# A gated delta rule on one core: the order of all engines' work around one (head, sequence) pair

## The chip, the core and the metric

The kernel runs on one core of a Trainium2 chip. The time is the device time of that core in microseconds. The core has TensorE (PE; its weight loads are shown as PEld), VectorE (DVE), ScalarE (ACT), GpSimd (POOL) and SyncE (SP), which here only starts DMA transfers. Each engine executes its own list of instructions strictly in the order in which the kernel writes them, and the lists are tied together by semaphores.

## The reference

Input x has 8 sequences of 512 rows with 256 features. The computation is:

```
h  = layernorm(x)
q,k,v = silu(causal_conv4(h @ Wqkv)) in 16 heads of 128;  z = h @ Wz
beta = sigmoid(h @ Wb);  g = -exp(A_log) * softplus(h @ Wa + dt_bias)
q, k = l2norm(q) / sqrt(128), l2norm(k)
for t:  M = exp(g_t) M;  M = M + k_t (v_t - k_t M) beta_t;  o_t = q_t M
o  = rmsnorm(o) * norm_w * silu(z);  x = x + layernorm(o @ Wout)
x  = x + layernorm(W3 relu(W2 relu(W1 layernorm(x) + b1) + b2) + b3)
```

## The kernel before

There are three stages. The first (`normalise_and_gate`) normalises x, writes its transpose as a high and a low float32r part to DRAM, and computes beta and the decays. The second (`delta_heads`) is nine tenths of the time and the only one that the change touches. The third (`mlp`) closes the attention part and computes the multilayer part.

The second stage treats 128 pairs of a head and a sequence, head by head. For each pair p it does, on TensorE unless said otherwise:

- `project(Q, K, V, Z)`: each is six float32r products of 128x512 (high times high, high times low, low times high, in two halves of 256 features), into two PSUM banks used in turn. ScalarE (`convolve(i, p)`) and VectorE (`convolve(i, 1..3, p)`, L740) apply the four taps, ScalarE (`activate`) the silu.
- `turn_q`, `turn_k`, `turn_v`, `turn_o`: four float32 transposes each. ScalarE sums squares (`squares`) and copies (`take_k`, `take_v`). VectorE's `norms`, `inverse_norm` (L767), `state_scale` (L779, f = f * beta, 128x4, both operands in SBUF) and `q_norm` (L773) make the small scale factors; GpSimd's `k_norm` (L556) is a power over 128x4.
- `grams`: the products k k' and q k' within four chunks of 128 rows. VectorE's `decay_b` (L790, L791) and `decay_qk` (L799, L800) apply the decays that `decays` (L751, a scan over two SBUF operands) made for this pair.
- The inverse of a triangular 128x128 matrix per chunk: GpSimd's `scale_b` (L508) and `unit_diagonal` (L515), ScalarE's `high_b` (L660), GpSimd's `low_b` (L522) and `first_transpose` (L529), and then levels 0 to 6, each with a group `z_level` or `z_first` and a group `tx_level` of short fp16 products (128x64), a `mask_level` (L817) on VectorE and a `take` (L666, L667) on ScalarE. `residual` (fp16 products), VectorE's `residual` (L826, it writes yr), `correction` (fp16), ScalarE's `correction` (L674) and GpSimd's `inverse` (L570) refine it once.
- The recurrence over chunks c = 0 to 3: `from_state_k(c)` (L1042), VectorE's `rhs(c)` (L847 for c = 0, which reads v_tok and a block of zeros from SBUF and kn from `k_norm`; L852 for the others), `solve(c)` (L1035), ScalarE's `state_input(c)` (L609, it writes u), `state_update(c)` (L1065), VectorE's `state(c)` (L834, L836, it writes m) and `outputs(c)` (L1055, L1056). These are float32 products of 128x128. A float32 product is written as two instructions in the trace.
- `turn_o`, VectorE's `gated` (L870) and `out_sums` (L861), GpSimd's `out_norm` (L564), `out_project(0 and 1)` (L1074), ScalarE's `take_sum` (L697) and GpSimd's `add(0 and 1)` (L577), which adds the pair's share to `attn`.
- GpSimd also multiplies the decays into k and q (`scale_kq`, L541, two instructions) and k_tok (`scale_k_tok`, L549), and in every second pair it splits a quarter of the next head's weights into high and low parts (`split`, L500 and L502).

What sets the order: each engine has one loop `for a in range(PAIRS + LAST_STAGE)`, with its work written out in a fixed order. A pair is spread over several iterations: `grams(a)` and `solve(0, a - 2)` stand in the same iteration, so four or five pairs are under way at once. Helper `real(p)` leaves out pairs that don't exist at both ends. The order of these lists is written out by hand in the kernel; there is no planner in it. `wait(engine, semaphore, count)` stands at the head of each helper. SyncE loads, for pair a + 1, the transposed input and the decays, and once a head the next weights; its list is not touched.

Of the kernel before, what the change touches and what calls it, by code (L numbers as in the profile page):

```python
# [27 lines left out]
EPS = 1e-6  # L28
RESIDUAL_SCALE = 1024.0
Q, K, V, Z = range(4)  # L30
LAST_STAGE = 4


def level_masks():
# [286 lines left out]
def delta_heads(nc, ctx, sem, buf, w_heads, conv_w, norm_w, w_out, identity, masks,  # L321
# [106 lines left out]
    def real(p):  # L428
        return 0 <= p < PAIRS
# [24 lines left out]
    with nc.Block() as block:  # L454
# [32 lines left out]
        def _(pool):  # L487
# [16 lines left out]
            def scale_b(p):  # L504
                if real(p):
                    wait(pool, b_raw, p + 1)
                    wait(pool, f_ready, p + 1)
                    nc.gpsimd.tensor_tensor(b32[:, :, :], b32[:, :, :],  # L508
                                            of(f, p)[:, :].unsqueeze(2).to_broadcast([P, CH, P]),
                                            ALU.mult).then_inc(b_scaled, 1)  # L510
# [22 lines left out]
            def scale_kq(p):  # L533
                if real(p):
                    pool.wait_ge(of(cum_in, p), DMA * (p // 4 + 1))
                    wait(pool, gram, p + 1)
                    wait(pool, turned_q, p + 1)
                    wait(pool, turned_k, p + 1)
                    for i in range(2):
                        part = of(kq, p)[:, i, :]  # L540
                        last = nc.gpsimd.tensor_tensor(part, part, of(cum, p)[:, :], ALU.mult)  # L541
                    last.then_inc(ks_ready, 1)

            def scale_k_tok(p):
                if real(p):
                    wait(pool, k_tok_ready, p + 1)
                    wait(pool, e_ready, p + 1)
                    part = of(k_tok, p)[:, :, :]
                    nc.gpsimd.tensor_tensor(part, part, of(e, p)[:, :, P - 1:P].to_broadcast([P, CH, P]),  # L549
                                            ALU.mult).then_inc(kts_ready, 1)  # L550
# [30 lines left out]

            for a in range(PAIRS + LAST_STAGE):
                head, slot = a // NSEQ, a % NSEQ
                scale_b(a - 1)
                unit_diagonal(a - 1)
                scale_k_tok(a - 2)
                out_norm(a - 4)
                first_transpose(a - 1)
                scale_kq(a - 1)
                low_b(a - 1)  # L590
                add(1, a - 4)
                k_norm(a - 1)
                inverse(a - 2)
                add(0, a - 4)
                if slot % 2:
                    split(slot // 2, head + 1)

        @block.scalar
        def _(act):
# [99 lines left out]
                    last.then_inc(part_taken[i], 1)  # L699

            for a in range(PAIRS + LAST_STAGE):
                activate(V, a - 1)
                take_out(a - 4)
                take(3, a - 2)
                take_v(a - 1)
                out_squares(a - 4)
                high_b(a - 1)
                state_input(1, a - 3)
                take(4, a - 2)
                gates(a - 1)  # L710
                take_sum(0, a - 4)
                take(5, a - 2)
                take_sum(1, a - 4)
                convolve(Q, a)
                take(1, a - 1)
                convolve(K, a)
                state_input(2, a - 3)
                take(6, a - 2)
                activate(Q, a)
                take(2, a - 1)  # L720
                squares(turned_q, 1, sums_q, a)
                activate(K, a)
                convolve(V, a)
                correction(a - 2)
                squares(turned_k, 0, sums_k, a)
                state_input(3, a - 3)
                take_k(a)
                state_input(0, a - 2)

        @block.vector  # L730
        def _(dve):
# [138 lines left out]
                    nc.vector.tensor_tensor(yt[:, :], flat(tr), of(gate, p)[:, :], ALU.mult).then_inc(yt_ready, 1)  # L870

            for a in range(PAIRS + LAST_STAGE):
                convolve(V, 3, a - 1)
                mask_level(3, a - 2)
                inverse_norm(a - 1)
                decay_b(a - 1)
                state_scale(a - 1)
                state(0, a - 3)
                rhs(0, a - 2)
                q_norm(a - 1)  # L880
                decay_qk(a - 1)
                rhs(1, a - 3)
                mask_level(4, a - 2)
                gated(a - 4)
                out_sums(a - 4)
                mask_first(a - 1)
                mask_level(5, a - 2)
                decays(a)
                mask_level(1, a - 1)
                state(1, a - 3)  # L890
                mask_level(6, a - 2)
                rhs(2, a - 3)
                convolve(Q, 1, a)
                convolve(Q, 2, a)
                mask_level(2, a - 1)
                convolve(Q, 3, a)
                convolve(K, 1, a)
                convolve(K, 2, a)
                state(2, a - 3)
                convolve(K, 3, a)  # L900
                residual(a - 2)
                rhs(3, a - 3)
                convolve(V, 1, a)
                convolve(V, 2, a)
                norms(a)

        @block.tensor
        def _(pe):
# [167 lines left out]
                    last.then_inc(outp[i], 1)  # L1076

            for a in range(PAIRS + LAST_STAGE):
                outputs(3, a - 4, signal=o_done)
                state_update(0, a - 3)  # L1080
                tx_level(3, a - 2)
                turn_v(a - 1)
                project(Z, a - 1)
                from_state_k(1, a - 3)
                z_level(4, a - 2)
                turn_o(a - 4)
                solve(1, a - 3)
                out_bank_free(a - 3)
                outputs(0, a - 3)
                tx_level(4, a - 2)  # L1090
                z_first(a - 1)
                out_project(0, a - 4)
                state_update(1, a - 3)
                z_level(1, a - 1)
                z_level(5, a - 2)
                out_project(1, a - 4)
                tx_level(5, a - 2)
                project(Q, a)
                z_level(6, a - 2)
                tx_level(1, a - 1)  # L1100
                from_state_k(2, a - 3)
                project(K, a)
                solve(2, a - 3)
                z_level(2, a - 1)
                tx_level(6, a - 2)
                outputs(1, a - 3)
                tx_level(2, a - 1)
                outputs(2, a - 3)
                residual(a - 2)
                state_update(2, a - 3)  # L1110
                turn_q(a)
                project(V, a)
                from_state_k(3, a - 3)
                correction(a - 2)
                turn_k(a)
                solve(3, a - 3)
                grams(a)
                solve(0, a - 2)
                z_level(3, a - 1)


def at(n):
# [242 lines left out]
```

## Time and profile before

| what | us |
|---|---|
| median of 3 runs (lowest, highest) | 2854.52 (2853.42, 2854.96) |
| the profiled execution | 2854.09 |
| its span, first to last instruction | 2852.0 |
| PE busy | 2673.0 (94%) |
| DVE busy | 2272.5 (80%) |
| ACT busy | 2150.6 (75%) |
| POOL busy | 1907.4 (67%) |

Busy times are sums over the whole span. The second stage runs from about 110 to 2565 us. A row of the timeline below gives the start in us from the span's start, the time from the first start to the last end of the merged instructions, the engine, the line of the kernel, the operation, the output and inputs by the program's names, the shape and the count; in square brackets stand the idle time before it and what released it. Ends of PE's products are modelled, and the next one starts before the last has ended, so the time that a group takes is read from start to start.

### The profile page before, as it was taken

To read this page: it belongs to the slowest core of one execution; us is meant where nothing else is said; L and a number is where in the kernel's file an instruction comes from. 1 tells how busy PE (TensorE), PEld (TensorE's weight loads), DVE (VectorE), ACT (ScalarE), POOL (GpSimd) and SP (SyncE) were. 2 spreads that over 40 slices of the span, in tenths; PEclk is the share of its full clock that TensorE was granted. 3 is DMA by queue.
4 is the path that set the end of the run, shared out by engine and by line. 5 is a ranking of instruction groups with operands and counts; after the bars stand their busy time and mean duration, and the time that the engine had idled before them with its cause. 6 is when DMAs were issued, how large, how long until landed. Compare 5 with 4: busy or idle time off the path is not lost. (4 is left out here: it accounts for less than half of the span.)

```text
span 2852.0 us, 70166 instructions
## 1 busy us (share of the span) xinstructions
PE 2673.0 (94%) x23604; PEld 2262.3 (79%) x23604; DVE 2272.5 (80%) x5006; ACT 2150.6 (75%) x7286; POOL 1907.4 (67%) x1707
## 2 busy tenths in 40 slices
PE   3399999999999999999999999999999999986998
PEld 2288888888888888888888888888888888873554
DVE  5588888888888888888888888888888888843433
ACT  2388888888888888888888888888888888861221
POOL 2267777787777777777777777787777777751000
PEclk9699999999999999999999999999999999987999
DMA  5322222222222222222222222222222222201000
GB/s 193 124 90 98 90 91 74 98 90 92 78 86 97 90 90 75 97 90 97 70 95 90 97 80 85 90 97 89 70 96 90 98 78 80 94 1 61 29 29 30
DMA packets 78568, 241.79 MB, mean 85 GB/s; under 512 B 8336, under 2 KB 21520, under 8 KB 61584
## 3 DMA queue, kind: packets, MB, share of 16 engines
q1 hardware_dynamic: 78224, 237.41, 23.6%
q8 instruction: 191, 3.13, 0.4%
q14 instruction: 153, 1.25, 0.1%
HBM read 223.75 MB, written 13.63 MB: 83 GB/s over the span
## 5 line engine op out<-in xcount | busy, mean ns | idle before, releaser
L740 DVE SCALAR_TENSOR_TENSOR conv<-pj,cw,conv 128x511 f32<-128x511 f32 (+2 forms) x1152 | 847.1, 744 | 54.3 <-ACT conv L615 40.3
L928 PE MATMUL pj<-xt,w_hi 128*128 128x512 f32 x2048 | 684.3, 415 | 23.3 <-DVE wo L734 23.3
L541 POOL TENSOR_TENSOR kq<-kq,cum 128x512 f32<-128x512 f32 x256 | 442.1, 1745 | 0.0
L570 POOL TENSOR_TENSOR inv<-inv,x 128x512 f32<-128x512 f32 x128 | 148.3, 1159 | 411.3 <-ACT inv L674 411.3
L928 PE MATMUL pj<-xt,w_lo 128*128 128x512 f32 x1024 | 404.7, 395 | 0.0
L928 PEld LDWEIGHTS pj<-xt,w_hi 128*128 128x128 f32 x2048 | 348.7, 190 | 69.5 <-DVE wo L734 23.7
L615 ACT ACTIVATE conv<-pj,cw 128x512 f32<-128x512 f32 x384 | 266.3, 693 | 124.3 <-PE pj L928 114.6
L817 DVE TENSOR_TENSOR y<-bk,mask 128x256 f16<-128x256 f32 x512 | 216.0, 422 | 166.8 <-PE bk L994 160.5
L577 POOL TENSOR_TENSOR attn<-attn,part 128x512 f32<-128x512 f32 x256 | 326.7, 1277 | 10.8 <-ACT part L697 10.8
L634 ACT ACTIVATE squares_out<-tr 128x128 bf16<-128x128 f32 x1024 | 273.7, 300 | 46.3 <-PE tr L935 46.3
L1074 PE MATMUL pj<-wo,yt 128*128 128x256 f32 x1024 | 284.0, 400 | 0.8 <-DVE yt L870 0.8
L666 ACT ACTIVATE x<-bk 128x256 f16<-128x256 f32 x512 | 196.5, 384 | 114.1 <-PE bk L1008 102.9
L975 PE MATMUL g<-kq 128*128 128x256 f32 x1024 | 242.2, 379 | 0.0
L1035 PE MATMUL st<-r,inv 128*128 128x128 f32 x1024 | 215.9, 292 | 24.1 <-DVE r L852 21.1
L634 ACT ACTIVATION_READ_ACCUMULATOR squares_out<-tr 128x1 f32 x1024 | 235.2, 231 | 0.0
L609 ACT ACTIVATE u<-st,f 128x128 f32<-128x128 f32 x512 | 195.6, 382 | 52.0 <-PE st L1035 34.9
L928 PEld LDWEIGHTS pj<-xt,w_lo 128*128 128x128 f32 x1024 | 193.0, 189 | 45.1
L1035 PEld LDWEIGHTS st<-r,inv 128*128 128x128 f32 x1024 | 163.3, 189 | 82.3 <-DVE r L852 47.4
L697 ACT ACTIVATE part<-pj,oc 128x256 f32<-128x256 f32 x512 | 215.7, 477 | 7.9 <-PE pj L1074 7.8
L508 POOL TENSOR_TENSOR b<-b,f 128x512 f32<-128x512 f32 x128 | 139.7, 1091 | 104.6 <-DVE f L779 104.6
L975 PEld LDWEIGHTS g<-kq 128*128 128x128 f32 x1024 | 184.8, 190 | 19.8
L1056 PE MATMUL op<-u,qk 128*128 128x128 f32 x1024 | 198.5, 276 | 0.1
(160 smaller groups left out, 7505.4 us busy)
## 6 DMA issues: line engine op xcount, KB each, us to landing
xt<-xt_scratch SPq DMA_DIRECT2D x128, 1024.0 KB, 4.8
decay<-decay_scratch SPq DMA_DIRECT2D x128, 256.0 KB, 5.3
cum<-cumdecay_scratch SPq DMA_DIRECT2D x128, 256.0 KB, 5.5
w_raw<-in_w_heads SPq DMA_DIRECT2D x16, 512.0 KB, 7.3
xt_scratch<-xt_hi SPq DMA_DIRECT2D x8, 512.0 KB, 2.8
xt_scratch<-xt_lo SPq DMA_DIRECT2D x8, 512.0 KB, 3.8
res<-in_x SPq DMA_DIRECT2D x8, 512.0 KB, 4.7
out<-yo SPq DMA_DIRECT2D x8, 512.0 KB, 3.1
```

The lines of the kernel that those rows point to most:

```text
L541: last = nc.gpsimd.tensor_tensor(part, part, of(cum, p)[:, :], ALU.mult)
L577: nc.gpsimd.tensor_tensor(rows, rows, part[:, 2 * i:2 * i + 2, :], ALU.add).then_inc(added[i], 1)
L615: nc.scalar.activation(conv[:, i, :], pj[:, i % 2, :], ACT.Copy, scale=cw[:, i, p // NSEQ, TAPS - 1:TAPS]).then_inc(pre[i], 1)
L634: last = nc.scalar.activation(squares_out[:, row, c, :], tr[:, c, :], ACT.Square, accum_out=of(sums, p)[:, row, c:c + 1])
L697: last = nc.scalar.activation(part[:, c, :], pj[:, i, DM * (c % 2):DM * (c % 2) + DM], ACT.Copy, scale=oc[:, c:c + 1])
L740: nc.vector.scalar_tensor_tensor(out=conv[:, i, j:SEQ], in0=pj[:, i % 2, 0:SEQ - j], scalar=cw[:, i, p // NSEQ, TAPS - 1 - j:TAPS - j], in ...
L817: nc.vector.tensor_tensor(y[level][:, :, :].rearrange("p c (g two w) -> p c g two w", two=2, w=w)[:, :, :, 0, :], ps[:, 0:CH * HALF].rearr ...
L928: last = nc.tensor.matmul(pj[:, i % 2, :], w[:, kt, cols], x_[:, kt, :], start=(n == 0), stop=(n == 3 * KT - 1))
L975: last = nc.tensor.matmul((g0, g1)[c // 2][:, cols], of(kq, p)[:, 0, chunk(c)], of(kq, p)[:, :, chunk(c)], start=True, stop=True)
L1035: nc.tensor.matmul(st[:, 1, :], of(inv, p)[:, c, :], r[:, c, :], start=True, stop=True).then_inc(w_done[c], 1)
L1056: mm = nc.tensor.matmul(op[:, c, :], of(qk, p)[:, c, :], u[:, c, :], start=(c == 0), stop=True)
L1074: last = nc.tensor.matmul(pj[:, i, DM * (c % 2):DM * (c % 2) + DM], yt[:, chunk(c)], wo[:, p // NSEQ, :], start=True, stop=True)
```

## The change

Only the order of the calls within the four loops changes, and LAST_STAGE. All four loops are also rotated by the same part of an iteration, so that an iteration now begins at `tx_level(5)` on TensorE; for that, most indices are one larger. Seen from one pair, as a cycle, these moves are left:

- TensorE: `solve(2)` from behind `project(K)` to behind `project(Q)`; `from_state_k(2)` from before `project(K)` to behind `out_project(1)`; `state_update(2)` from behind `residual` to before `outputs(2)`, and `outputs(2)` before `tx_level(2)`; `outputs(0)` from behind `solve(1)` to between `from_state_k(3)` and `correction`, where it is the last but one output of its pair; `state_update(1)` before `out_project(0)`; `z_level(5)` before `z_level(1)`.
- ScalarE: `take(5)` behind `take_sum(1)`; `state_input(2)` before `take(1)`.
- VectorE: `mask_level(6)` behind `rhs(2)`; `state(2)` before K's second tap; `inverse_norm` before `mask_level(3)`; `rhs(0)` before `state(0)`; `state(1)` before `mask_level(5)`.
- GpSimd: the new cycle is `scale_b`, `unit_diagonal`, `add(0)`, `out_norm`, `first_transpose`, `split`, `scale_kq` (of the pair before), `scale_k_tok`, `low_b`, `inverse`, `add(1)`, `k_norm`. Before it was `scale_b`, `unit_diagonal`, `scale_k_tok`, `out_norm`, `first_transpose`, `scale_kq` (of the same pair), `low_b`, `add(1)`, `k_norm`, `inverse`, `add(0)`, `split`.

```diff
--- before.py
+++ after.py
@@ -28,7 +28,7 @@
 EPS = 1e-6
 RESIDUAL_SCALE = 1024.0
 Q, K, V, Z = range(4)
-LAST_STAGE = 4
+LAST_STAGE = 5
 
 
 def level_masks():
@@ -581,19 +581,19 @@
 
             for a in range(PAIRS + LAST_STAGE):
                 head, slot = a // NSEQ, a % NSEQ
+                scale_k_tok(a - 2)
+                low_b(a - 2)
+                inverse(a - 3)
+                add(1, a - 5)
+                k_norm(a - 2)
                 scale_b(a - 1)
                 unit_diagonal(a - 1)
-                scale_k_tok(a - 2)
+                add(0, a - 5)
                 out_norm(a - 4)
                 first_transpose(a - 1)
-                scale_kq(a - 1)
-                low_b(a - 1)
-                add(1, a - 4)
-                k_norm(a - 1)
-                inverse(a - 2)
-                add(0, a - 4)
                 if slot % 2:
                     split(slot // 2, head + 1)
+                scale_kq(a - 2)
 
         @block.scalar
         def _(act):
@@ -699,6 +699,22 @@
                     last.then_inc(part_taken[i], 1)
 
             for a in range(PAIRS + LAST_STAGE):
+                take(5, a - 3)
+                convolve(Q, a - 1)
+                state_input(2, a - 4)
+                take(1, a - 2)
+                convolve(K, a - 1)
+                take(6, a - 3)
+                activate(Q, a - 1)
+                take(2, a - 2)
+                squares(turned_q, 1, sums_q, a - 1)
+                activate(K, a - 1)
+                convolve(V, a - 1)
+                correction(a - 3)
+                squares(turned_k, 0, sums_k, a - 1)
+                state_input(3, a - 4)
+                take_k(a - 1)
+                state_input(0, a - 3)
                 activate(V, a - 1)
                 take_out(a - 4)
                 take(3, a - 2)
@@ -709,23 +725,7 @@
                 take(4, a - 2)
                 gates(a - 1)
                 take_sum(0, a - 4)
-                take(5, a - 2)
                 take_sum(1, a - 4)
-                convolve(Q, a)
-                take(1, a - 1)
-                convolve(K, a)
-                state_input(2, a - 3)
-                take(6, a - 2)
-                activate(Q, a)
-                take(2, a - 1)
-                squares(turned_q, 1, sums_q, a)
-                activate(K, a)
-                convolve(V, a)
-                correction(a - 2)
-                squares(turned_k, 0, sums_k, a)
-                state_input(3, a - 3)
-                take_k(a)
-                state_input(0, a - 2)
 
         @block.vector
         def _(dve):
@@ -870,13 +870,27 @@
                     nc.vector.tensor_tensor(yt[:, :], flat(tr), of(gate, p)[:, :], ALU.mult).then_inc(yt_ready, 1)
 
             for a in range(PAIRS + LAST_STAGE):
+                mask_level(6, a - 3)
+                convolve(Q, 1, a - 1)
+                convolve(Q, 2, a - 1)
+                mask_level(2, a - 2)
+                convolve(Q, 3, a - 1)
+                convolve(K, 1, a - 1)
+                state(2, a - 4)
+                convolve(K, 2, a - 1)
+                convolve(K, 3, a - 1)
+                residual(a - 3)
+                rhs(3, a - 4)
+                convolve(V, 1, a - 1)
+                convolve(V, 2, a - 1)
+                norms(a - 1)
                 convolve(V, 3, a - 1)
+                inverse_norm(a - 1)
                 mask_level(3, a - 2)
-                inverse_norm(a - 1)
                 decay_b(a - 1)
                 state_scale(a - 1)
+                rhs(0, a - 2)
                 state(0, a - 3)
-                rhs(0, a - 2)
                 q_norm(a - 1)
                 decay_qk(a - 1)
                 rhs(1, a - 3)
@@ -884,25 +898,11 @@
                 gated(a - 4)
                 out_sums(a - 4)
                 mask_first(a - 1)
+                state(1, a - 3)
                 mask_level(5, a - 2)
                 decays(a)
                 mask_level(1, a - 1)
-                state(1, a - 3)
-                mask_level(6, a - 2)
                 rhs(2, a - 3)
-                convolve(Q, 1, a)
-                convolve(Q, 2, a)
-                mask_level(2, a - 1)
-                convolve(Q, 3, a)
-                convolve(K, 1, a)
-                convolve(K, 2, a)
-                state(2, a - 3)
-                convolve(K, 3, a)
-                residual(a - 2)
-                rhs(3, a - 3)
-                convolve(V, 1, a)
-                convolve(V, 2, a)
-                norms(a)
 
         @block.tensor
         def _(pe):
@@ -1076,6 +1076,30 @@
                     last.then_inc(outp[i], 1)
 
             for a in range(PAIRS + LAST_STAGE):
+                tx_level(5, a - 3)
+                project(Q, a - 1)
+                solve(2, a - 4)
+                z_level(6, a - 3)
+                tx_level(1, a - 2)
+                project(K, a - 1)
+                z_level(2, a - 2)
+                tx_level(6, a - 3)
+                out_bank_free(a - 4)
+                outputs(1, a - 4)
+                state_update(2, a - 4)
+                outputs(2, a - 4)
+                tx_level(2, a - 2)
+                residual(a - 3)
+                turn_q(a - 1)
+                project(V, a - 1)
+                from_state_k(3, a - 4)
+                outputs(0, a - 4)
+                correction(a - 3)
+                turn_k(a - 1)
+                solve(3, a - 4)
+                grams(a - 1)
+                solve(0, a - 3)
+                z_level(3, a - 2)
                 outputs(3, a - 4, signal=o_done)
                 state_update(0, a - 3)
                 tx_level(3, a - 2)
@@ -1085,38 +1109,14 @@
                 z_level(4, a - 2)
                 turn_o(a - 4)
                 solve(1, a - 3)
-                out_bank_free(a - 3)
-                outputs(0, a - 3)
                 tx_level(4, a - 2)
                 z_first(a - 1)
+                state_update(1, a - 3)
                 out_project(0, a - 4)
-                state_update(1, a - 3)
+                z_level(5, a - 2)
                 z_level(1, a - 1)
-                z_level(5, a - 2)
                 out_project(1, a - 4)
-                tx_level(5, a - 2)
-                project(Q, a)
-                z_level(6, a - 2)
-                tx_level(1, a - 1)
                 from_state_k(2, a - 3)
-                project(K, a)
-                solve(2, a - 3)
-                z_level(2, a - 1)
-                tx_level(6, a - 2)
-                outputs(1, a - 3)
-                tx_level(2, a - 1)
-                outputs(2, a - 3)
-                residual(a - 2)
-                state_update(2, a - 3)
-                turn_q(a)
-                project(V, a)
-                from_state_k(3, a - 3)
-                correction(a - 2)
-                turn_k(a)
-                solve(3, a - 3)
-                grams(a)
-                solve(0, a - 2)
-                z_level(3, a - 1)
 
 
 def at(n):
```

## Rows read from the trace of the kernel before

**Rows 1.** Busy us (instructions) by engine, clock, DMA share and GB/s, 600 to 1000.

```profile
600.00:1000.00 400.00, 396.69 (x3784) 349.29 (x3783) 348.60 (x742) 343.26 (x1185) 309.53 (x276) 1.00 0.24 87
```

**Rows 2.** Timeline, PE, three Grams: start us, length us, engine, line, operation.

```profile
1003.22 1.89 PE L975 MATMUL g<-kq 128*128 128x256 f32 x8
...
1022.28 1.89 PE L975 MATMUL g<-kq 128*128 128x256 f32 x8
...
1040.95 1.89 PE L975 MATMUL g<-kq 128*128 128x256 f32 x8
```

**Rows 3.** Timeline, PE, solve(1); turn_o and solve(1) a period later.

```profile
1009.54 0.49 PE L1035 MATMUL st<-r,inv 128*128 128x128 f32 x2 [0.33 <-DVE r L852]
...
1027.64 0.63 PE L935 MATMUL tr<-ident,o 128*128 128x128 f32 x4
1028.20 0.49 PE L1035 MATMUL st<-r,inv 128*128 128x128 f32 x2
```

**Rows 4.** Timeline, DVE, state_scale twice, then rhs(0) and rhs(1).

```profile
1006.59 0.57 DVE L779 SCALAR_TENSOR_TENSOR f<-f,beta 128x4 f32<-128x4 f32 x1
...
1025.65 0.16 DVE L779 SCALAR_TENSOR_TENSOR f<-f,beta 128x4 f32<-128x4 f32 x1
...
1025.92 1.22 DVE L847 SCALAR_TENSOR_TENSOR r<-v_tok,kn,zeros 128x128 f32<-128x128 f32 x1
...
1027.80 0.34 DVE L852 SCALAR_TENSOR_TENSOR r<-v_tok,kn,st 128x128 f32<-128x128 f32 x1
```

**Rows 5.** Timeline, POOL; then groups (x count, busy us, mean ns, idle before) of POOL.

```profile
1006.41 0.73 POOL L502 TENSOR_TENSOR w_lo<-w_raw,w_hi 128x256 fp32r<-128x256 f32 x1
...
1022.66 1.16 POOL L570 TENSOR_TENSOR inv<-inv,x 128x512 f32<-128x512 f32 x1 [3.18 <-ACT inv L674]
1023.77 1.28 POOL L577 TENSOR_TENSOR attn<-attn,part 128x512 f32<-128x512 f32 x1
1025.95 1.04 POOL L508 TENSOR_TENSOR b<-b,f 128x512 f32<-128x512 f32 x1 [0.90 <-DVE f L779]
...
L541 POOL TENSOR_TENSOR kq<-kq,cum 128x512 f32<-128x512 f32 x256 | 442.1, 1745 | 0.0
...
L556 POOL TENSOR_TENSOR kn<-k,halves 128x4 f32<-128x4 f32 x128 | 130.4, 1019 | 0.0
```

**Rows 6.** Timeline, PE, outputs(1) as two product pairs, tx(2); state_update(2), turn_q.

```profile
1035.87 0.47 PE L1055 MATMUL op<-m,kq 128*128 128x128 f32 x2
1036.17 0.39 PE L1056 MATMUL op<-u,qk 128*128 128x128 f32 x2
1036.39 0.28 PE L1005 MATMUL g<-y,x 128*128 128x64 f16 x4
...
1037.60 0.44 PE L1065 MATMUL st<-u,k_tok 128*128 128x128 f32 x2
1037.88 0.60 PE L935 MATMUL tr<-ident,kq 128*128 128x128 f32 x4
```

**Rows 7.** Timeline, PE, from_state_k(3), correction, turn_k, solve(3).

```profile
1021.04 0.38 PE L1042 MATMUL st<-m,kq 128*128 128x128 f32 x2
1021.29 0.40 PE L1025 MATMUL bk<-x,yr 128*128 128x128 f16 x4
1021.57 0.66 PE L935 MATMUL tr<-ident,kq 128*128 128x128 f32 x4
1022.06 0.39 PE L1035 MATMUL st<-r,inv 128*128 128x128 f32 x2
```

**Rows 8.** Timeline, ACT u(1), then PE out_project(0), state_update(1), z(1).

```profile
1028.72 0.37 ACT L609 ACTIVATE u<-st,f 128x128 f32<-128x128 f32 x1 [0.28 <-PE st L1035]
...
1029.20 1.08 PE L1074 MATMUL pj<-wo,yt 128*128 128x256 f32 x4
1030.12 0.38 PE L1065 MATMUL st<-u,k_tok 128*128 128x128 f32 x2
1030.34 0.28 PE L994 MATMUL g<-t,b_hi 128*128 128x64 f16 x4
```

## Prediction

> **What bounds the kernel now.** I read the busy shares by stretch first. In the head stage TensorE is busy 396.69 of 400 us at full granted clock, VectorE 348.60, ScalarE 343.26, GpSimd 309.53 [rows 1]. So TensorE sets the time here, and a change of order pays only where it takes idle or exposed time out of TensorE's own stream. The reader should look next at how long one pair takes on TensorE, from one Gram product to the next: 19.06 us, then 18.66 us [rows 2], in turn. The weight split runs in every second pair (odd slots in the code), and the two lengths alternate with it: GpSimd's L502 stands in the long one [rows 5]. The mean is 18.86 us. 127 such periods lie between 128 Grams; the first three are shorter (the pipeline fills), so a saving counts about 124 times.
>
> Where do the 0.40 us come from? In the long period TensorE idles 0.33 us ahead of solve(1), released by VectorE's `rhs(1)` [rows 3]. On VectorE, `state_scale` (L779, both operands in SBUF, 128x4) took 0.57 us there and 0.16 us in the short period [rows 4]. It started at 1006.59 and ended at 1007.16; GpSimd's second split instruction (L502) ran from 1006.41 to 1007.14 [rows 5]. VectorE stood still until GpSimd was through. Everything behind it (`decay_qk`, `rhs(1)`) came 0.41 us late, and solve(1) with it. The same happens in the short period between `rhs(0)` (L847, 1.22 us, 1025.92 to 1027.14) and `scale_b` (L508, 1025.95 to 1026.99) [rows 4, 5]. Even the short period is not free of a wait: turn_o takes 0.56 us up to solve(1) [rows 3], while turn_k, itself slightly held up, takes 0.49 [rows 7]; unheld I put turn_o at 0.47, so 0.09 is a wait.
>
> The Trainium skill, page "SBUF — State Buffer", section "Who interferes with whom", says that a VectorE instruction with two SBUF inputs contends with a GpSimd instruction that reads SBUF, and that issue order decides which one blocks. The 0.57 against 0.16 agrees. It speaks against a part of this change, since `k_norm` now runs on GpSimd when `state_scale` is due; the sum below with that rule is 2827 us and without it 2844.
>
> **The parts of the change.** Each loop is also rotated, so LAST_STAGE grows to 5; in terms of one pair the order stays cyclic, and I cost the extra, mostly empty iteration at nothing (bounds -2 to +2 us, by add(1), a 1.28 us instruction [rows 5], once or twice at the end).
>
> *TensorE, groups that change their neighbour.* outputs(1) shows the price: its first product pair, behind the fp16 group tx(6), takes 0.30 us, its second, behind float32, 0.22 [rows 6]. So float32 behind short fp16 costs 0.08. outputs(2) now stands behind a float32 group: -0.08. state_update(2) takes 0.28 behind the residual [rows 6]; behind outputs(1) it takes the 0.22 of a pair: -0.06. turn_q moves behind fp16 instead: +0.01. state_update(1) and out_project(0) swap places: the first gains the 0.06 that the second loses, 0. from_state_k(2) leaves the place between tx(1) and project(K), and then the projection stands behind fp16: the 0.08 changes owner, 0. Sum -0.13 us per period.
>
> *TensorE, waits around the correction.* outputs(0) now fills the place between from_state_k(3) and correction. Today correction's start waits for VectorE's yr, and turn_k for ScalarE's activate(K): the steps are 0.25, 0.28 and 0.49 us [rows 7]. With 0.22 more work ahead, they should be 0.22, 0.22 and 0.44: -0.14 us (bounds -0.14 to 0, if VectorE and ScalarE come just as much later). I take -0.14, because VectorE's next work on Q and K does not wait for anything new.
>
> *TensorE, a new wait.* state_update(1) moves ahead of out_project(0), and outputs(0) no longer stands between. It needs u(1). With S the start of solve(1): ScalarE starts u at S + 0.52 and takes 0.37 [rows 3, 8], so state_update(1) can start at S + 0.91. Today out_project(0) starts at S + 1.00 [rows 3, 8], with solve(1), outputs(0), tx(4) and z_first before it; without outputs(0), a pair of 0.22, TensorE is there at S + 0.78. out_project(0), today 0.92 with state_update(1) at 0.22 behind it [rows 8], is queued behind the wait. The wait of 0.13, a first load exposed (0.30 instead of 0.22, as outputs(1) shows) and out_project at 0.87 give 1.30 against 1.14: +0.16 us. Bounds +0.05 (only the exposed load) and +0.25.
>
> Together: from solve(1) to the next Gram there are 12.75 us today (1028.20 to 1040.95 [rows 2, 3]); new 12.75 - 0.13 - 0.14 + 0.16 = 12.64.
>
> *GpSimd and VectorE, the start of solve(1).* S is today 5.92 us after the Gram (short) and 6.32 (long). The split moves behind first_transpose, where VectorE's only instruction with both operands in SBUF is the scan `decays`, which should be issued before the split. Today it stands in the same place ahead of scale_kq and gets its turn first: it is scale_kq that is stretched, to a mean of 1.75 us where add takes 1.28 [rows 5]. So I take the 0.40 of the long period as gone. (If the split did come first, `decays` and behind it `mask_level(1)` and `rhs(2)` would be up to 1.1 us late in every second pair, ahead of solve(2), which has some 0.2 in hand: at most 0.45 us per period, more than all that is gained. I count this into B.) What is late next? The new GpSimd order is inverse, add(1), k_norm, scale_b without a gap. inverse starts 0.38 after the Gram, add 1.11 later, and add's end is at 2.77 [rows 2, 5]; k_norm takes 1.02 [rows 5]. With the overlap of 0.04 that inverse and add show, k_norm ends at 3.75, and scale_b, which today waits 0.90 us idle and starts at 3.67, is no longer early. inverse follows ScalarE's correction; the shorter steps ahead of the Gram bring that up to 0.11 forward relative to it. I take 0.06: k_norm ends at K = 3.69 (bounds 3.63 and 3.75). `state_scale` would be issued at 3.3 to 3.4 and stands until K, as it does behind the split. `rhs(0)` needs kn of the same k_norm, so it starts at K + 0.05. scale_b follows at K + 0.16, as today 0.14 after f is ready, and is held 0.09 by rhs(0): its 1.04 ends at K + 1.29. `q_norm` stands until then; from there to the end of decay_qk and rhs(1) it is 1.02 us (today 1026.99 to 1028.20 are 1.21, of which rhs(0)'s own 0.19 falls away). S = K + 2.31 = 6.00. Bounds: 5.85 (K = 3.63, rhs(0) done before scale_b, +2.22) and 6.13 (K = 3.75, +2.38).
>
> Period = 6.00 + 12.64 = 18.64 us against 18.86: -0.22. Times 124: -27 us. VectorE, ScalarE and GpSimd keep 2.4, 2.7 and 4.3 us idle per period (400 us hold 21.2 periods [rows 1]), so no engine becomes the bound by its work; scale_kq one pair later is still done a good 10 us before from_state_k(1) asks for it, and low_b and scale_k_tok likewise. The profiled execution took 2854.1 us (span 2852.0 and 2.1 around it), the median of the runs is 2854.5. 2854.1 - 27 = 2827 us.
>
> **Rivals.**
> A, k_norm (128x4) does not hold VectorE. Then scale_b starts right at K, ahead of rhs(0), which stands behind it to K + 1.17; m(0) comes late and from_state_k(1) with it, S = K + 2.45 = 6.14. Period 18.78, -0.08: 2844 us. For it: no row shows a pow instruction beside such a VectorE one. Against it: L502, with half the elements of a usual GpSimd operand, does hold it.
>
> B, slower: the chain inverse, add(1), k_norm, scale_b takes over at its worst. inverse stays at 0.38 (K 3.75), state(0), now behind rhs(0), lets from_state_k(1) start 0.1 to 0.3 late, and S = 6.28. It decides from S = 6.22 on, since 6.22 + 12.64 is today's mean; the long period's price of today would be paid in every period. 18.92, +0.06: 2854.1 + 8 = 2862 us. For it: GpSimd's gap of 0.90 us ahead of scale_b is what the new order uses up. Against: it needs rhs(0) to be issued behind scale_b, while only the 0.16 that scale_b waits for f speaks on that.
>
> C, inverse comes earlier than I grant and TensorE alone sets the period: S cannot be under 5.83 (turn_o unheld), 5.83 + 12.64 = 18.47, -0.39: 2806 us. For it: the pairs' chain through ScalarE has several short waits that may all shrink. Against: it needs rhs(0) and k_norm both out of the way.
>
> **How the numbers follow.** Forecast 0.55, A 0.13, B 0.16, C 0.16. The forecast's own bounds: period 18.49 to 18.77, so 2808 to 2843. A measurement here can tell about 0.2% (5.7 us) from no change. Faster takes the forecast, C and most of A, less what lies inside 5.7 us: 0.73. Same, 0.11, comes from the edge of the forecast, of A and of B. Slower 0.16, B. The range goes from 2805, near C, to 2858, which leaves out B's upper part and a deeper gain.
>
> **What would show each step.** L779 at about 0.4 to 0.57 us in every period and not only in every second one: `state_scale` stands behind k_norm. L847 near 0.34 us instead of 1.22 and L508 near 1.1: rhs(0) goes first. Equal periods with and without a split: the 0.40 is gone. outputs(2)'s first product at 0.22 to the next and not 0.30; no wait at correction and turn_k; a wait of ScalarE's u ahead of state_update(1) of 0.13. I am wrong if the periods still alternate, if solve(1) starts over 6.2 us after the Gram, or if TensorE shows a new idle of over 0.2 us at a place not named here.

## The result, and the profile after

The changed kernel took 2888.89 us (median of 4 runs, 2886.68 to 2889.59) against 2853.97 us for the kernel before on the same chip (4 runs): ratio 1.0121, 95% interval 1.0104 to 1.0139. It is 1.2% slower. The forecast was 2827 us, and the time lies outside the range. The span of the profiled execution grew from 2852.0 to 2884.6 us.

The first view is the busy time by stretch of the kernel after, in the same stretch as [rows 1]:

```profile
600.00:1000.00 400.00, 394.30 (x3723) 341.85 (x3724) 347.72 (x731) 336.36 (x1175) 303.44 (x272) 1.00 0.24 86
```

TensorE is still the busiest engine, but it idles 5.7 us here, where it idled 3.3. The loss is spread evenly: the 123 periods from the fifth Gram product to the last take 2353.5 us, 2321.0 before. That is +32.5 of the +32.6 us. Before, periods of 18.66 and 19.06 us alternated [rows 2]; now nearly every one is 19.13. So the alternation went, as forecast, and the common length is above both.

The timeline of TensorE in one period after shows where it waits (start us, length us, engine, line, operation; what released it in brackets; the same places as [rows 2, 3, 6 to 8]):

```profile
1262.44 1.89 PE L975 MATMUL g<-kq 128*128 128x256 f32 x8
...
1267.50 0.49 PE L1042 MATMUL st<-m,kq 128*128 128x128 f32 x2
...
1268.88 0.49 PE L1035 MATMUL st<-r,inv 128*128 128x128 f32 x2 [0.29 <-DVE r L852]
...
1269.82 0.49 PE L1065 MATMUL st<-u,k_tok 128*128 128x128 f32 x2
1270.15 1.03 PE L1074 MATMUL pj<-wo,yt 128*128 128x256 f32 x4
...
1277.27 0.39 PE L1055 MATMUL op<-m,kq 128*128 128x128 f32 x2
1277.49 0.39 PE L1056 MATMUL op<-u,qk 128*128 128x128 f32 x2
...
1280.45 0.39 PE L1056 MATMUL op<-u,qk 128*128 128x128 f32 x2
1280.68 0.39 PE L1025 MATMUL bk<-x,yr 128*128 128x128 f16 x4
1280.90 0.61 PE L935 MATMUL tr<-ident,kq 128*128 128x128 f32 x4
1281.34 0.39 PE L1035 MATMUL st<-r,inv 128*128 128x128 f32 x2
1281.57 0.60 PE L975 MATMUL g<-kq 128*128 128x256 f32 x2
```

Subtract the Gram's 1262.44. from_state_k(1) starts at 5.06 and solve(1) at 6.44, after an idle time of 0.29 that VectorE's `rhs(1)` ends. Before, solve(1) started at 5.92 or 6.32 [rows 2, 3]. From solve(1) to the next Gram it is 12.69 us, 12.75 before. TensorE's own list did get a little shorter; the period got longer ahead of solve(1), and only there.

Who makes `rhs(1)` late? VectorE in the same period (compare [rows 4]):

```profile
1265.71 0.15 DVE L779 SCALAR_TENSOR_TENSOR f<-f,beta 128x4 f32<-128x4 f32 x1
1266.21 1.03 DVE L847 SCALAR_TENSOR_TENSOR r<-v_tok,kn,zeros 128x128 f32<-128x128 f32 x1 [0.35 <-POOL kn L556]
1267.17 0.28 DVE L834 COPY m<-st 128x128 f32<-128x128 f32 x1
1267.37 0.53 DVE L773 SCALAR_TENSOR_TENSOR q<-k 128x4 f32<-128x4 f32 x1
1267.82 0.41 DVE L799 TENSOR_TENSOR qk<-g,e 128x256 f32<-128x256 f32 x1
...
1268.49 0.33 DVE L852 SCALAR_TENSOR_TENSOR r<-v_tok,kn,st 128x128 f32<-128x128 f32 x1
```

and GpSimd (compare [rows 5]):

```profile
1265.07 1.02 POOL L556 TENSOR_TENSOR kn<-k,halves 128x4 f32<-128x4 f32 x1
1266.06 1.04 POOL L508 TENSOR_TENSOR b<-b,f 128x512 f32<-128x512 f32 x1
1267.25 0.64 POOL L515 TENSOR_SCALAR_AFFINE_SELECT b<-b 128x512 f32<-128x512 f32 x1
1267.85 1.27 POOL L577 TENSOR_TENSOR attn<-attn,part 128x512 f32<-128x512 f32 x1
```

Read the two together. `state_scale` (L779) takes its plain 0.15 us although `k_norm` (L556) is running. `rhs(0)` (L847) waits for kn, is issued at 1266.21, after `scale_b` (L508, 1266.06), and stands until that ends at 1267.10; its own work then takes it to 1267.24. Then `state(0)` (L834) follows, where the old order had `q_norm` (L773). So `q_norm` is issued only at 1267.37. By then `unit_diagonal` (L515) has started, at 1267.25, and `q_norm` takes 0.53 instead of 0.15 us: it ends at 1267.90, with L515 at 1267.89. `decay_qk`, `rhs(1)` and solve(1) come behind it. The groups of VectorE over the whole run (count, busy us, mean ns) say that this is the rule and that the split no longer touches `state_scale`:

```profile
L773 DVE SCALAR_TENSOR_TENSOR q<-k 128x4 f32<-128x4 f32 x128 | 68.1, 532 | 0.0
L779 DVE SCALAR_TENSOR_TENSOR f<-f,beta 128x4 f32<-128x4 f32 x128 | 19.8, 155 | 0.0
```

### The profile page after: what moved, and what is told of

Read it like the earlier page. It is cut to its first block and busy times, and to the rows that moved or that the text cites. A ratio compares the mean times of both kernels' runs of the same rounds, so it can differ in the third digit from the quotient of the medians.

```text
span 2884.6 us, 70166 instructions
## 1 busy us (share of the span) xinstructions
PE 2690.7 (93%) x23604; PEld 2244.7 (78%) x23604; DVE 2298.4 (80%) x5006; ACT 2131.6 (74%) x7286; POOL 1898.6 (66%) x1707
## 5 line engine op out<-in xcount | busy, mean ns | idle before, releaser
L541 POOL TENSOR_TENSOR kq<-kq,cum 128x512 f32<-128x512 f32 x256 | 387.1, 1533 | 0.0
L1074 PE MATMUL pj<-wo,yt 128*128 128x256 f32 x1024 | 277.4, 394 | 0.8 <-DVE yt L870 0.8
L1035 PEld LDWEIGHTS st<-r,inv 128*128 128x128 f32 x1024 | 170.5, 189 | 92.8 <-DVE r L852 69.0
L564 POOL TENSOR_TENSOR oc<-oms,halves 128x4 f32<-128x4 f32 x128 | 130.4, 1019 | 104.4 <-DVE oms L861 104.2
L667 ACT ACTIVATE t<-bk 128x256 f16<-128x256 f32 x512 | 198.9, 388 | 0.0
```

The source lines that it names most:

```text
L667: nc.scalar.activation(half(of(t16, p), level, 0), packed(ps, level, 0), ACT.Copy).then_inc(tx_ready[level], 1)
L1035: nc.tensor.matmul(st[:, 1, :], of(inv, p)[:, c, :], r[:, c, :], start=True, stop=True).then_inc(w_done[c], 1)
L1074: last = nc.tensor.matmul(pj[:, i, DM * (c % 2):DM * (c % 2) + DM], yt[:, chunk(c)], wo[:, p // NSEQ, :], start=True, stop=True)
```

## The experiments

Theory T: the loss is this hold-up of `q_norm` on VectorE. Rival R: `k_norm` in front of `scale_b` makes `scale_b` late and is the cause by itself. Rival P: TensorE's new order costs the time. Spans are of the profiled executions; ratios are against the kernel before on the same chip, with 95% intervals. Indices are as in the loops after, in e3, e4 and e9 as in those before. Where a gain is counted by the 123 periods, it leaves out the stretches ahead of the fifth Gram and behind the last; the last one alone lies between 334 and 345 us from run to run, and puts some us into the differences of spans.

**e5: state(0) ahead of rhs(0) again.** One swap of the change undone.

```diff
-                rhs(0, a - 2)
                 state(0, a - 3)
+                rhs(0, a - 2)
                 q_norm(a - 1)
```

> The kernel after with one swap undone on VectorE: state(0) ahead of rhs(0) again, so that q_norm follows rhs(0) directly. Theory T (the loss is a hold-up on VectorE: q_norm, issued 4.93 us after the Gram, comes behind GpSimd's unit_diagonal, issued 4.80, and stands 0.38 us): rhs(0) still stands behind scale_b until 4.80, but q_norm is issued about 4.73, ahead of unit_diagonal, takes 0.15, and solve(1) starts at 5.86 and not 6.43. Period 18.56 us instead of 19.13: 2884.6 - 0.57 x 124 = span 2814. Rival R (k_norm in front of scale_b, and so scale_b itself, sets the start of solve(1)): no change, span 2884. Rival P (TensorE's new order costs the time): no change, 2884.

Measured: 2816.9 us, ratio 0.9877 (0.9861 to 0.9894), span 2815.3. VectorE, then GpSimd's L515, then TensorE in one period of e5:

```profile
1238.57 0.28 DVE L834 COPY m<-st 128x128 f32<-128x128 f32 x1
1238.99 1.03 DVE L847 SCALAR_TENSOR_TENSOR r<-v_tok,kn,zeros 128x128 f32<-128x128 f32 x1
1239.95 0.15 DVE L773 SCALAR_TENSOR_TENSOR q<-k 128x4 f32<-128x4 f32 x1
```

```profile
1240.03 0.64 POOL L515 TENSOR_SCALAR_AFFINE_SELECT b<-b 128x512 f32<-128x512 f32 x1
```

```profile
1235.23 1.89 PE L975 MATMUL g<-kq 128*128 128x256 f32 x8
...
1240.22 0.39 PE L1042 MATMUL st<-m,kq 128*128 128x128 f32 x2
...
1241.12 0.49 PE L1035 MATMUL st<-r,inv 128*128 128x128 f32 x2
...
1241.70 0.39 PE L984 MATMUL g<-ident,b_hi 128*128 128x128 f16 x4
1242.06 0.49 PE L1065 MATMUL st<-u,k_tok 128*128 128x128 f32 x2
1242.39 1.03 PE L1074 MATMUL pj<-wo,yt 128*128 128x256 f32 x4
...
1253.80 1.46 PE L975 MATMUL g<-kq 128*128 128x256 f32 x6
```

`rhs(0)` stands behind `scale_b` just as long (1.03 us), but `q_norm` is issued at 1239.95, 0.08 us ahead of `unit_diagonal`, and is free. solve(1) starts 5.89 us after the Gram instead of 6.44, and the period shown takes 18.57 (most take 18.59). One swap of two short instructions is worth 69 us of the span, 65 of them in the 123 periods. T stands; R and P, which expected no change, fall.

**e2: q_norm behind state_scale.** This leaves state(0) late and frees `q_norm` alone.

```diff
                 state_scale(a - 1)
+                q_norm(a - 1)
                 rhs(0, a - 2)
                 state(0, a - 3)
-                q_norm(a - 1)
```

> The kernel after with another single move on VectorE: q_norm right behind state_scale, ahead of rhs(0) and state(0), k_norm and the swap of rhs(0) and state(0) as in the change. Theory T (the hold-up of q_norm behind unit_diagonal is the loss): q_norm takes 0.15 us at 3.35; rhs(0) stands behind scale_b to 4.80, state(0) ends 5.01, decay_qk starts 4.93, rhs(1) 5.60 to 5.93, solve(1) at 5.99: period 18.69, span 2884.6 - 0.44 x 123 = 2830. Rival (what matters is that state(0) comes late, behind rhs(0), and from_state_k(1) with it): this order leaves state(0) late, so little is won, span 2870 to 2884.

Measured: 2844.3 us, ratio 0.9964 (0.995 to 0.9978), span 2840.7. The period is 18.77. So of the 0.54 us that e5 gains per period, 0.37 is the hold-up of `q_norm`; the other 0.17 comes from `state(0)` standing behind the held `rhs(0)`. TensorE's from_state_k(1), then decay_qk's second half and `rhs(1)` on VectorE, in one period of e2:

```profile
1247.87 0.49 PE L1042 MATMUL st<-m,kq 128*128 128x128 f32 x2
```

```profile
1248.07 0.41 DVE L800 TENSOR_TENSOR qk<-g,e 128x256 f32<-128x256 f32 x1
1248.48 0.35 DVE L852 SCALAR_TENSOR_TENSOR r<-v_tok,kn,st 128x128 f32<-128x128 f32 x1
```

from_state_k(1) reads what `state(0)` writes. It starts 5.06 us after the Gram instead of 5.00 in e5, and takes 0.49 instead of 0.39. `rhs(1)` reads its result and starts 0.61 after it (0.49 in e5), at 5.67 instead of 5.49. The expectation was 11 us too low: it let `rhs(1)` follow decay_qk at 5.60, with the overlap of 0.08 us that it has in the kernel after (1268.49 against the end at 1268.57), and did not count the longer from_state_k(1). In e2 `rhs(1)` starts without that overlap and 0.12 after from_state_k(1) ends; in e5 and e1, where it also waits for that result, it is 0.11.

**e10: a longer hold-up.** `q_norm` is moved to where GpSimd's add(0) runs.

```diff
-                q_norm(a - 1)
                 decay_qk(a - 1)
+                q_norm(a - 1)
                 rhs(1, a - 3)
```

> The kernel after with the suspected hold-up made longer: q_norm behind decay_qk, where it would be issued at about 5.6 us and GpSimd's add(0) (1.27 us long) is running. Theory T (a VectorE instruction with two SBUF inputs stands until the running GpSimd instruction ends, and rhs(1) and solve(1) stand behind it): decay_qk ends 5.67, q_norm is held to 6.68, rhs(1) ends 6.96, solve(1) at 7.02: period 19.72, span 2884.6 + 0.59 x 123 = 2957. If the order of q_norm doesn't matter, 2884.

Measured: 2959.4 us, ratio 1.0367 (1.035 to 1.0385), span 2957.1, period 19.72. `q_norm` on VectorE, add(0) on GpSimd and solve(1) on TensorE:

```profile
1299.98 1.11 DVE L773 SCALAR_TENSOR_TENSOR q<-k 128x4 f32<-128x4 f32 x1
```

```profile
1299.81 1.27 POOL L577 TENSOR_TENSOR attn<-attn,part 128x512 f32<-128x512 f32 x1
```

```profile
1301.41 0.49 PE L1035 MATMUL st<-r,inv 128*128 128x128 f32 x2 [0.89 <-DVE r L852]
```

`q_norm` takes 1.11 us and ends at 1301.09, with add(0) at 1301.08. Moving a 128x4 instruction that nobody on the path needs costs 72 us of span over the kernel after, purely by where it stands.

**e1: k_norm into GpSimd's gap.**

```diff
                 low_b(a - 2)
+                k_norm(a - 2)
                 inverse(a - 3)
                 add(1, a - 5)
-                k_norm(a - 2)
```

> The kernel after with one GpSimd instruction moved: k_norm between low_b and inverse, where GpSimd idles 3.96 us, and no longer in front of scale_b. T: scale_b starts 0.14 after f is ready, at 3.56; rhs(0) doesn't wait for kn, is issued at 3.35 ahead of scale_b and takes 0.34; q_norm is issued about 3.9, stands behind scale_b to 4.75; solve(1) at 5.83 to 5.95, period 18.5 to 18.65, span 2808 to 2826. R: the same. P: no change, 2884.

Measured: 2816.6 us, ratio 0.9877 (0.986 to 0.9893), span 2817.5. Here kn is ready early, `rhs(0)` is issued ahead of `scale_b`, and `q_norm`, though it now stands behind `scale_b`, and decay_qk are through 0.2 us before `rhs(1)` gets what from_state_k(1) makes. `q_norm` is held longer here than in the kernel after (0.81 us on average against 0.53), but from an earlier start, and at no cost: what counts is when the hold-up ends. Both cures end at the same period, 18.59: solve(1) again starts at 5.89. What sets it now is from_state_k(1), `rhs(1)`, solve(1), 0.90 us from start to start.

**e3 and e4: parts of the change in the kernel before.** e3 moves the split only; e4 also puts `k_norm` in front of `scale_b`.

```diff
                 first_transpose(a - 1)
+                if slot % 2:
+                    split(slot // 2, head + 1)
                 scale_kq(a - 1)
                 low_b(a - 1)
                 add(1, a - 4)
                 k_norm(a - 1)
                 inverse(a - 2)
                 add(0, a - 4)
-                if slot % 2:
-                    split(slot // 2, head + 1)
```

and in e4 as well:

```diff
-                k_norm(a - 1)
                 inverse(a - 2)
                 add(0, a - 4)
+                k_norm(a - 1)
```

> The kernel before with one thing of the change: the weight split in the middle of GpSimd's list, behind first_transpose, all else as before. All theories: state_scale takes 0.16 us in every period, all periods are 18.66 us, the 0.40 of every second one is gone: 2852.0 - 60 x 0.40 = span 2828. If the split in the middle costs something itself (scale_kq late), periods with a split are longer than the others.

> The kernel before with the split in the middle and k_norm last in GpSimd's list, right in front of scale_b, as in the kernel after; VectorE's list as before, q_norm right behind rhs(0). R (k_norm in front of scale_b is what costs): the period rises to about 19.1, span 2880. T: rhs(0) stands behind scale_b to about 4.9, q_norm slips in ahead of unit_diagonal and is not held; solve(1) about 5.96 instead of 5.92, period 18.70, span 2832. P says nothing on this run.

Measured: e3 2830.1 us, ratio 0.9923 (0.9906 to 0.9939), span 2830.2, nearly all periods 18.66; e4 2834.2 us, ratio 0.994 (0.9924 to 0.9957), span 2832.8, periods 18.70. The split's new place gains 22 us by itself. `k_norm`'s new place costs some 3 us in the old VectorE order (the two intervals overlap), and not the 50 that R expected: it does harm only together with `rhs(0)` ahead of `state(0)`.

**e12: TensorE's gain, one part of it.** e5 with outputs(2) and state_update(2) behind fp16 groups again. VectorE's `state(2)` also goes back behind K's second tap, where it stood with them; what that move does by itself no run shows.

```diff
+                convolve(K, 2, a - 1)
                 state(2, a - 4)
-                convolve(K, 2, a - 1)
                 ...
                 outputs(1, a - 4)
-                state_update(2, a - 4)
-                outputs(2, a - 4)
                 tx_level(2, a - 2)
+                outputs(2, a - 4)
                 residual(a - 3)
+                state_update(2, a - 4)
                 turn_q(a - 1)
```

> e5 with one part of TensorE's order undone: outputs(2) behind tx(2) and state_update(2) behind the residual again (and state(2) behind K's second tap on VectorE, where it stood with them). By the sum of the prediction both products stand behind fp16 groups again, +0.08 and +0.06, less 0.01 at turn_q: period 18.58 + 0.13 = 18.71, span 2815.3 + 0.13 x 123 = 2831. Rival (something else on TensorE, a wait behind it, takes the difference up, as it did in e6): no change, 2815.

Measured: 2834.1 us, ratio 0.993 (0.9913 to 0.9947), span 2834.1, 18.8 us over e5; 14.9 of them lie in the 123 periods, 0.12 a period. The term of -0.13 in the prediction was right.

**e6, e7: out_project(0) ahead of state_update(1) again.** Both also have e5's swap, and e7 has e1's move as well.

```diff
-                state_update(1, a - 3)
                 out_project(0, a - 4)
+                state_update(1, a - 3)
```

> e5 (state(0) ahead of rhs(0)) with one TensorE swap of the change undone: out_project(0) ahead of state_update(1) again. With the wait for u(1) the three groups z_first, state_update(1), out_project(0) take 0.36 + 0.33 + 0.87 = 1.56 us in e5; without it 0.23 + 0.92 + 0.22 = 1.37. Period 18.58 - 0.19 = 18.39, span 2815 - 23 = 2792. Rival (TensorE is no longer alone the bound at that pace; ScalarE's or VectorE's results for turn_q, correction or turn_k come late): period 18.5, span 2806 or no change.

> e6 with k_norm between low_b and inverse on GpSimd as well. In e5 and e1 solve(1) started at the same 5.89 us, set by the chain from_state_k(1), rhs(1), solve(1), 0.89 long, and not by scale_b any more. If so this run equals e6 within 2 us, 2792. If GpSimd's scale_b is the next bound at the faster pace, it is up to 6 us faster than e6.

Measured: e6 2816.8 us, ratio 0.987 (0.9854 to 0.9887), span 2812.1; e7 2816.1 us, ratio 0.9865 (0.9848 to 0.9881), span 2814.6. Both periods are 18.57. This missed: 23 us were expected; 3 came in the span, 2 in the 123 periods, and no gain over e5 is clear of the noise. e7 equals e6, as expected of it, but at e6's time and not at the 2792 us forecast. z_first, out_project(0) and state_update(1) on TensorE in e6, then `gated` on VectorE:

```profile
1239.99 0.39 PE L984 MATMUL g<-ident,b_hi 128*128 128x128 f16 x4
1240.35 1.13 PE L1074 MATMUL pj<-wo,yt 128*128 128x256 f32 x4
1241.31 0.38 PE L1065 MATMUL st<-u,k_tok 128*128 128x128 f32 x2
```

```profile
1239.61 0.68 DVE L870 TENSOR_TENSOR yt<-tr,gate 128x512 f32<-128x512 f32 x1
```

z_first still takes 0.36 us up to the next group; in the kernel before it took 0.22. out_project(0) starts 0.06 after `gated` ends at 1240.29: one wait took the place of the other. In this place two results, u(1) and yt, both depend on `rhs(1)` being early.

**e8: outputs(0) between turn_o and solve(1).** e6, with outputs(0) taken from ahead of the correction.

```diff
-                out_bank_free(a - 4)
                 outputs(1, a - 4)
                 ...
                 from_state_k(3, a - 4)
-                outputs(0, a - 4)
                 ...
                 turn_o(a - 4)
+                out_bank_free(a - 3)
+                outputs(0, a - 3)
                 solve(1, a - 3)
```

> e6 with outputs(0) of the pair between turn_o and solve(1), where TensorE waits about 0.1 us for rhs(1) and then shows a bare weight load of 0.1; it no longer stands between from_state_k(3) and correction. solve(1) starts about 0.13 later instead of 0.22; in front of correction and turn_k the waits of the kernel before (0.14 together) come back if VectorE's yr and ScalarE's activate(K) are the bound there: period 18.39 + 0.13 - 0.22 + 0.14 = 18.44, span 2798. If the waits don't come back: 18.30, span 2781.

Measured: 2813.6 us, ratio 0.9855 (0.9839 to 0.9871), span 2812.7, periods 18.54. This is the fastest version run, and 1.45% below the kernel before, but its interval overlaps those of e5, e1, e6 and e7. Its period lies 0.03 below e6's; the expectation, 2798 or 2781, started from the period that e6 had missed. The wait in front of solve(1) goes, and part of the one in front of the correction comes back (from_state_k(3) takes 0.34 us up to the correction where it needs 0.22).

**e9, e11: TensorE's order exchanged as a whole.** e9 is e3 with TensorE's new list (and mask_level(6) behind rhs(2) on VectorE); e11 is the kernel after with TensorE's old list.

In both, LAST_STAGE is 5, and besides TensorE's list and the split of e3 one move within a loop is left, e9's on VectorE:

```diff
-                mask_level(6, a - 2)
                 rhs(2, a - 3)
+                mask_level(6, a - 2)
```

> e3 (the kernel before with the split in the middle) with TensorE's whole new order, and mask_level(6) behind rhs(2) on VectorE, without which that order can't run; the other engines as before. It shows what TensorE's new order is worth alone. The sum of the prediction (-0.13 - 0.14 + 0.16 = -0.11 us a period) gives 18.55, span 2830 - 14 = 2816. What e3 and e5 show from solve(1) to the next Gram (12.74 and 12.69) gives -0.05, 18.61, span 2824. Rival P (TensorE's new order is what made the kernel slower): over 2850.

> The kernel after with TensorE's old order, the other three engines as in the change. Theory T: the hold-up of q_norm stays, solve(1) starts about 6.43 us after the Gram, and from there it is 12.74 to the next: period 19.17, span 2889. Rival P: back at 18.66 to 18.86, span 2830 to 2852.

Measured: e9 3079.2 us, ratio 1.0792 (1.0774 to 1.081); e11 3104.4 us, ratio 1.0882 (1.0864 to 1.09). Both missed far (2816 or 2824, and 2889, were expected): the expectations counted TensorE's list by itself. The waits of TensorE from 500 to 2000 us (us in total, times, longest), e9 and then e11, show new ones of a microsecond or more a period:

```profile
PEld st L1042 <- DVE m L836: 130.1, 72, 1.9
PE st L1042 <- DVE m L836: 101.2, 72, 1.5
```

```profile
PEld g L994 <- ACT t L667: 86.1, 72, 1.2
PE g L994 <- ACT t L667: 72.6, 72, 1.0
```

In e9 from_state_k(2) stands for `state(1)`, which in VectorE's old list comes behind `decays`; in e11 z_level(2) stands for `take(1)`. The lists of the four engines are tuned to one another, and a whole list can't be judged in another company. P is therefore not tested by these two. It falls by e5, which has TensorE's new list and is fast. One thing they do show: solve(1) starts 5.89 us after the Gram in e9 and 6.40 in e11. The late start goes with the other engines' lists, not with TensorE's.

## Why the prediction was wrong

By its own steps:

- *The split.* Right. The alternation is gone, `state_scale` is 0.155 us throughout, and e3 gives the 22 us alone (24 by 60 times 0.40). `decays` did get its turn ahead of the split; it is the cast that is held, its mean 1.26 us and not the 0.40 of the kernel before; periods with and without a split are equally long all the same:

```profile
L500 POOL CAST w_hi<-w_raw 128x256 fp32r<-128x256 f32 x64 | 80.4, 1257 | 3.5 <-DMA w_raw<-in_w_heads 3.5
```

- *Neighbours on TensorE.* Right: outputs(2)'s first pair takes 0.22 us in the timeline above, and e12 measures 0.12 for the -0.13.
- *The waits around the correction, and the new wait.* Nearly right. outputs(0), correction and turn_k take 0.23, 0.22 and 0.44. The wait for u(1) is there: state_update(1) starts 0.94 us after solve(1), forecast 0.91, and takes 0.33, forecast 0.30. From solve(1) to the next Gram 12.64 was forecast and 12.69 measured.
- *K, the end of k_norm.* Right: 3.65 (1265.07 + 1.02 - 1262.44), forecast 3.69.
- *From K to solve(1).* Wrong, and this is the step that failed. It put S at K + 2.31, or K + 2.45 if `k_norm` didn't hold `state_scale` (rival A). It didn't (L779 above), so the forecast's own case was gone and A's first half came true: `scale_b` ran at once and `rhs(0)` stood behind it to K + 1.15, forecast 1.17. But then S was K + 2.79, which gives the 6.44, over the 6.2 that the prediction named as a sign of being wrong. The working had `q_norm` standing behind `scale_b` in every case and going free when that ended. It did not ask what GpSimd runs next. With `state(0)` between `rhs(0)` and `q_norm`, `q_norm` came 0.12 us after the start of `unit_diagonal`, and stood 0.38. Where `q_norm` is out of the way, A's sum holds: in e2 S is K + 2.43 (6.07), and the time is the 2844 us that A gave, faster than before.
- *Rival B* had the outcome (18.92 and 2862 us; measured 19.13 and 2889) and the threshold (slower from S = 6.22 on), but not the mechanism. It priced a late `state(0)`, which is a third of what e5 gets back (0.17 of 0.54 us), and not the second hold-up.

The balance per period: 18.87 before; -0.20 for the split; -0.06 from solve(1) to the Gram; +0.52 for solve(1) at 6.44 against 5.92: 19.13, as measured.

The Trainium skill ("SBUF — State Buffer", section "Who interferes with whom") says that a VectorE instruction with two SBUF inputs contends with a GpSimd instruction that reads SBUF. The runs agree for `scale_b`, `unit_diagonal`, add and the split, which hold it until their end. They differ for `k_norm`: it reads two SBUF operands and `state_scale`, issued 0.64 us after it started, is not held; nor is `q_norm` in e2, 0.72 us after.

## What to carry to other kernels

When GpSimd and VectorE both run long lists, place each VectorE instruction with two SBUF operands against the GpSimd instruction that will be running when it is issued, and against the one after that; if it misses the gap between two, by 0.12 us here, it pays the rest of the next one. Tiny instructions (here 128x4) are the ones to look at: `q_norm` takes 0.15 us by itself and up to 1.11 when held, and in e2 it could simply stand elsewhere. And judge a new order by where its latest wait starts, not by the sum of what each list saves: here the list on the busiest engine got better and the kernel slower.

## What was not expected of the hardware

- A GpSimd power over 128x4 takes 1.02 us and yet did not hold VectorE's `state_scale` (0.155 us), while `unit_diagonal`, which is only 0.64 us long, held `q_norm` for all that was left of it. Whether the power holds VectorE in its first half no run here shows: no such VectorE instruction was issued less than 0.58 us after its start (e8's `state_scale`).
- The hold-up works in both directions and follows the order of issue: `rhs(0)` 0.16 us behind `scale_b` takes 1.03 us in e5; 0.23 ahead of it, in e1, it takes 0.34. Closer than 0.03 us the profile's starts don't tell who goes first: in the kernel before, `rhs(0)` starts 0.01 to 0.03 us ahead of `scale_b` in 125 of the 128 periods [rows 4, 5], and is held in 89 of them and free in 36.
